# The product of state and C in two steps, one per half of the channels, in a kernel for a Mamba, GRU and two feed-forward blocks

## What is computed

```python
def step(hstate, inp):
    dt_s, B_s, C_s, u_s = inp
    dA = jnp.exp(dt_s[..., None] * A)
    hstate = dA * hstate + (dt_s * u_s)[..., None] * B_s[:, None, :]
    y = jnp.einsum('bdn,bn->bd', hstate, C_s)
    return (hstate, y)
...
y = ys.transpose(1, 0, 2) + u * Dskip
y = y * jax.nn.silu(z)
return x + y @ W_out
```

## Time and profile before

| | |
|---|---|
| median of 3 runs | 854.37 us (851.23 to 859.19) |
| the profiled execution | 853.03 us |
| its span, first to last instruction | 851.2 us |
| busy: PE, DVE, ACT, POOL | 701.9, 678.1, 640.0, 585.1 us |
| mean granted TensorE clock | 0.91 of 2.4 GHz |

### The profile page before, as it was taken

One profiled execution on the slowest core, in us unless ns is written; L12 is line 12 of the kernel. 1 busy time (PEld: TensorE's weight loads), 2 busy tenths in 40 slices (PEclk: granted clock), 3 DMA queues, 4 the chain that ended last, 5 costly groups with the idle time before them and its releaser, 6 DMA issues. The chain is left out here.

```text
span 851.2 us, 12456 instructions
## 1 busy us (share of the span) xinstructions
PE 701.9 (82%) x4060; PEld 591.1 (69%) x4060; DVE 678.1 (80%) x1059; ACT 640.0 (75%) x964; POOL 585.1 (69%) x375
## 2 busy tenths in 40 slices
PE   5554666799789997899689978999789968997975
PEld 5443555678677886688667867688678857886764
DVE  3699988979987998999997998799879987752231
ACT  5777878697889879987999788987897587426313
POOL 3398768787779687878876887968796567415312
PEclk9786776999999998999999999999899979998996
DMA  5522121111111211122112211211102110000000
GB/s 139 167 60 60 51 65 59 52 50 63 38 52 46 78 39 50 44 63 58 50 41 62 63 38 52 58 55 43 57 28 75 50 50 25 1 1 2 13 1 12
DMA packets 35185, 42.79 MB, mean 50 GB/s; under 512 B 7457, under 2 KB 17074, under 8 KB 35122
## 3 DMA queue, kind: packets, MB, share of 16 engines
q1 hardware_dynamic: 35122, 42.00, 16.8%
HBM read 39.63 MB, written 2.36 MB: 49 GB/s over the span
## 5 line engine op out<-in xcount | busy, mean ns | idle before, releaser
L502 POOL TENSOR_TENSOR inflow<-dtu,b_all 128x1024 f32<-128x1024 f32 x127 | 307.5, 2423 | 74.7 <-DVE state L1075 46.7
L1075 DVE TENSOR_TENSOR_SCAN state<-dA,inflow 128x512 f32<-128x512 f32 x256 | 298.3, 1207 | 23.9 <-ACT dA L836 23.2
L836 ACT ACTIVATE dA<-dt,decay_c 128x512 f32<-128x512 f32 x256 | 170.3, 686 | 48.9 <-DVE state L1075 48.1
L1092 DVE TENSOR_TENSOR state<-state,c_ps 128x1024 f32<-128x1024 f32 x128 | 155.6, 1216 | 22.0 <-PE c_ps L1377 17.9
L1386 PE MATMUL y_ps<-ident,state 128*128 128x128 f32 x1024 | 149.1, 294 | 26.8 <-DVE state L1092 26.7
L1386 PEld LDWEIGHTS y_ps<-ident,state 128*128 128x128 f32 x1024 | 131.5, 153 | 43.7 <-DVE state L1092 32.1
L1273 PE MATMUL work<-in_hi,wzh_hi 128*128 128x512 f32 x256 | 103.9, 406 | 1.8 <-POOL in_lo L664 1.7
L1274 PE MATMUL work<-in_hi,wzh_lo 128*128 128x512 f32 x256 | 101.0, 395 | 0.0
L1275 PE MATMUL work<-in_lo,wzh_hi 128*128 128x512 f32 x256 | 101.0, 395 | 0.0
L1377 PE MATMUL c_ps<-xd,pick 128*128 128x512 f32 x128 | 63.5, 496 | 43.6 <-DVE state L1092 43.2
L655 POOL TENSOR_TENSOR wide<-wide 128x512 f32<-128x512 f32 x48 | 61.1, 1273 | 32.1 <-ACT wide L883 29.8
(11 more groups left out here) (164 smaller groups left out, 1493.0 us busy)
## 6 DMA issues: line engine op xcount, KB each, us to landing
b_all<-b_scratch SPq DMA_DIRECT2D x128, 256.0 KB, 3.2
x_tok<-in_x SPq DMA_DIRECT2D x8, 256.0 KB, 3.8
out_x<-x_tok SPq DMA_DIRECT2D x8, 256.0 KB, 3.6
wide<-in_Wz SPq DMA_DIRECT2D x1, 1024.0 KB, 7.8
wide<-in_Wh SPq DMA_DIRECT2D x1, 1024.0 KB, 9.0
skip_f<-in_W SPq DMA_DIRECT2D x2, 256.0 KB, 4.2
dtu<-in_W_in SPq DMA_DIRECT2D x1, 256.0 KB
mixed<-in_w_up SPq DMA_DIRECT2D x1, 256.0 KB, 2.8
```

The costliest lines, as they stand in the source:

```text
L502: eng.tensor_tensor(inflow[:, n % 2, :, tok(b)], dtu[:, :, tok(b)], b_all[:, n % RING, tok(b)].unsqueeze(1).broadcast_to([P, HALVES, TO[b] ...
L836: act.activation(dA[:, h, tok(b)], dt[:, b % 2, h, tok(b)], ACT.Exp, scale=decay_c[:, h, n:n + 1]).then_inc(s_dA[h], 1)
L1075: dve.tensor_tensor_scan(state[:, g % 3, h, tok(b)], dA[:, h, tok(b)], inflow[:, n % 2, h, tok(b)], first, ALU.mult, ALU.add).then_inc(s_s ...
L1092: dve.tensor_tensor(state[:, g % 3, :, tok(b)], state[:, g % 3, :, tok(b)], c_ps[:, tok(b)].unsqueeze(1).broadcast_to([P, HALVES, TO[b] - ...
```

## The change

The product is made by two instructions, one per half, each with a semaphore of its own (`read_ready0`, `read_ready1`). The four transposes of a half wait for their own half only. `mix_cn`, which overwrites `c_ps`, waits for both.

```diff
-                                                 sem("read_ready"), sem("acc_done"))
+                                                 [sem("read_ready%d" % h) for h in range(HALVES)], sem("acc_done"))
...
-                dve.tensor_tensor(state[:, g % 3, :, tok(b)], state[:, g % 3, :, tok(b)],
-                                  c_ps[:, tok(b)].unsqueeze(1).broadcast_to([P, HALVES, TO[b] - FROM[b]]), ALU.mult
-                                  ).then_inc(s_read, 1)
+                for h in range(HALVES):
+                    dve.tensor_tensor(state[:, g % 3, h, tok(b)], state[:, g % 3, h, tok(b)], c_ps[:, tok(b)], ALU.mult
+                                      ).then_inc(s_read[h], 1)
...
-                wait(pe, s_read, STATE * b + n)
+                for h in range(HALVES):
+                    wait(pe, s_read[h], STATE * b + n)
...
                 g = STATE * b + n
-                pe.wait_ge(s_read, g + 1)
                 for h in range(HALVES):
+                    pe.wait_ge(s_read[h], g + 1)
                     for j in tiles(b):
                         last = pe.matmul(y_region(j, h), state[:, g % 3, h, cols(j)], ident[:, :], is_transpose=True,
```

## The result

The changed kernel takes 863.7 us (862.11 to 864.21, 4 runs), beside 856.1 us (851.23 to 859.19, 4 runs) for the kernel before in the same session. The ratio on record is 1.0104, with a 95% interval of 1.0077 to 1.0132; the plain quotient of these two medians, 1.0089, lies inside it. Timed again on another chip, beside some of the experiments, it gave 1.0110 (1.0089 to 1.0132). It is slower, by some 9 us. I had said 859 (850 to 868), with 0.69 for a change within 1%; it came out just beyond that.

What follows compares the result with a forecast made beforehand. DVE was taken to lead most of the time, other engines nearly as full. 853.03 + 0.95 + 5.2 + 0.5 - 1.6 = 858.1 us against the profiled execution, 859 as a median; range 850 to 868.

Steps and rivals of the forecast that it cites:

- The price of a pair on DVE: DVE, each step: two half products hold it 0.06 us longer than a whole one, 7.7 us over 128 steps.
- The rival in which a half holds DVE for its whole duration: DVE, all steps: nothing overlaps, 0.138 us per step, 17.7 us passed on in full, 870 us; chance 0.05.
- What of it reaches the end: Added DVE time passes on by DVE's busy share: +0.95 us in row 0, +5.2 in rows 1 to 6, +0.5 in row 7.
- The early transposes in rows 1 to 7 bring nothing: PE, rows 1 to 7: transposes there never wait for the product, so starting them earlier gains nothing.
- The early transposes in row 0 bring 1.6 us: PE, row 0: transposes starting earlier shorten DVE's waits for `c_ps`, by 1.6 us in sum.
- The second waits on PE: PE, ahead of transposes and the matmul into `c_ps`: no cost taken; at most 0.02 us on each of 256, about 5 us.
- Absorbed: DVE, rows 1 to 6: its delays fall into its own waits, only row 0's gain is left, 853 us; chance 0.15.
- Losses of DVE and PE adding up: 108 products ahead of 720 us: each delay paid twice, 0.12 us each, 13.0 us, giving 866 us; chance 0.14.
- its 0.095: Price in us per product from which the rival of added DVE and PE losses decides, at 863 us.
- The signs: Profile after: L1093 256 times at 0.68 us, DVE 8 to 17 us busier, row 0's gate within 1 us, rows 1-6 +5 us.
- the signs of being wrong: A gap before the second four transposes behind 112 us, a pair over 1.25 us, or row 0 over 3 us shorter.
- Slower by over 1%: Whole kernel: 0.25, from 0.07 of the forecast itself, 0.13 of losses adding up and 0.05 of whole durations.

Runs made afterwards that it cites:

- the quarters: Each product made in four DVE steps of 256 elements, where the kernel before has one and the change two; 1.0153 against the kernel before.
- short halves: The changed kernel with its half products over 480 of 512 tokens, so a pair holds DVE as long as a whole product; 1.0000 against the kernel before.
- `c_ps` first: Kernel before, products whole, with row 0's matmul into `c_ps` placed ahead of the transposes of the step before; 0.9985 against the kernel before.

## Why the prediction was right or wrong, point by point

- **The price of a pair on DVE: right.** I took 0.06 us between 0.05 and 0.07 from two pairs in the trace. It measured 0.07 in the changed kernel (1.20 against 1.13) and 0.065 per instruction in the quarters. Only one of the two pairs is the same operation, L1101, and it had given the 0.07; L1058 is a SCALAR_TENSOR_TENSOR. The rival in which a half holds DVE for its whole duration (870 us) is refuted, and with it my use of the rule of the Trainium skill (VectorE: DVE Perf Modes, "The DRAIN you can't avoid") that the next instruction does not start until the pipe has emptied. The same section adds that one that is not held starts earlier, and I had left that out. The trace fits the addition: the second half starts 0.60 us after the first, which lasts 0.68 (1.28 us for the two records together).
- **What of it reaches the end: right in kind, too small.** I passed on DVE's busy share: +5.7 us in rows 1 to 7. From row 0's gate to row 7's, three profiles with the products of before take 631.2, 628.8 and 630.3 us, the two of the changed kernel 636.1 and 639.6: +7.8 us in the mean. With short halves it is 631.8 us, so this goes with DVE's time. Yet it is not the added time of these rows alone: the two kernels that are changed in row 0 only take 633.4 and 634.3 us over the same stretch, 3 to 4 more than before, with not an instruction changed in it. The busy share as a measure of what is handed on is not borne out: by the table the share is anything from a quarter to one, and by rows from nothing to several times.
- **The early transposes in rows 1 to 7 bring nothing: right.** No wait for the product stands ahead of them there, before or after.
- **The early transposes in row 0 bring 1.6 us: wrong.** This is the step that failed, though the time came out inside the range. With 0.95 us for the halves I had row 0 0.6 us shorter; from the first product to the gate it takes 73.2 and 73.1 us against 71.8, 70.6 and 71.8 before: 1.7 us longer. The halves without early transposes make 1.3 of that (72.7 and 72.8 us in two profiles), which leaves a loss of 0.4 to the early transposes where I had a gain of 1.6. Two of the three short waits for `c_ps` went as worked out, and more than that came back elsewhere, at one place behind a grant of the full clock that came later. Moreover, as the run with `c_ps` first shows, all of row 0's waits for it together (3.3 us) are worth about 1.3 us (0.9985), not their length. I had taken the length of a wait for its worth, after noting that TensorE was at its lower clock there and without asking what moves that clock.
- **The second waits on PE: right at nothing.** 0.9986 for 256 of them.
- **The rivals.** Absorbed: refuted. Losses of DVE and PE adding up, 866 us: not borne out as a rule; 9 us of DVE time became 9 us of the kernel's, which is the price paid once, though row 4 alone paid two to four times its own. (Its sum left out the products of row 0: with 123 products in place of 108 it gives 868.) The 1% was reached with 0.07 us per product and not only from its 0.095 on, in part because row 0 lost where I had it gain: without that error the sum is 858.1 + 1.6 = 859.7 against the profiled execution, 861 against the median, which is in the range but still within the 1%. The other 2 us are the part passed on, of which a price of 0.07 in place of 0.06 accounts for 1.3 at most.
- **The signs.** L1093 stands there 256 times at 0.68 us, DVE's busy time by records is 8.4 us more, and the next instruction follows a pair after 1.20 us, as I had said. Two signs failed: row 0's gate stands 3.2 and 1.3 us later than 110.08 and not within 1 us, and from row 0's gate to row 6's the kernel takes 549.9 and 553.4 us against 542.8 to 543.5, which is 7 to 10 us more and not 5. None of the signs of being wrong came.
- **Chances.** Slower by over 1% had 0.25. The ratio of 1.0104 lies on the line; the interval reaches to both sides of it.

## What to carry to other kernels

Splitting an instruction so that its reader may start early pays only where the reader waits for this very instruction; look at the reader's place in its own list, and at what it has already waited for there. The price of one more instruction is the distance between starts in a row of neighbours, not a difference of durations (0.065 us here, against 0.14). Before a size of wait is booked as a gain, take that wait away by another route and time it; and to settle a cause, keep the whole change and take only the suspected cost out of it, as the short halves do.

## What the runs showed of the hardware that I had not expected

- An earlier start of PE's work can go with a slower PE. Where transposes began 0.6 us earlier, the granted clock rose at about 46 us and not at 43, in two profiles of two, and the next eight transposes took 1.91 us in place of 1.10. In the profile with `c_ps` first the clock rose late too. With the old order this happened in one of five.
- The clock's edges make part of the spread between profiles of one kernel: the same four matmuls ahead of the first scan took 3.78 us in one profile of the changed kernel and 1.98 in the other, and the first product behind them stood at 40.11 and 38.24 us.
- In the changed kernel's second profile the second product starts at 42.28 us although both scans had ended by 41.78 and the matmul into `c_ps`, by its record, by 41.38. What held it for 0.50 us is open; the profile names the scan. The same wait (0.49 or 0.50 us) stands in all four profiles of kernels with early transposes in row 0 and two instructions per product, and in none of the kernels with the old order of PE.
